# Attention and output projection in one program: the last unit's heads among the products of the first four head groups

## The chip, the cores and the metric

One core of a Trainium2 chip runs the whole program. Its engines work side by side and meet at semaphores: TensorE (PE: matmuls and transposes, results in PSUM banks of 128 x 512 floats), VectorE (DVE), ScalarE (ACT), GpSimd (POOL), and SyncE (SP), which issues the transfers from HBM. The metric is the device time of one execution in microseconds (us), the median of several.

## The reference, cut to what matters

Six residual blocks work on `x`, 8 batches of 32 tokens with 512 values each. The first and the fourth are cross attentions onto a context of 512 tokens per batch; the names of their tiles begin with `c0` and `c1`. One of them computes:

```python
q = (x_norm @ Wq)      # 32 heads of 128
k = (kv @ Wk)          # 8 key/value heads; c0: context and latents, c1: context
v = (kv @ Wv)
q, k = rms_norm(q), rms_norm(k)
probs = softmax(q @ k.T * scale)
out = probs @ v        # 256 tokens x 4096
x = x + out @ Wo       # 4096 x 512
```

The change touches the end of the attention and the last line.

## The kernel before, in words

A full-precision product is three matmuls (`mm3`, lines 51 to 55): each operand is split in a high part (a copy to the rounded type, by ScalarE) and a low part (the difference, by VectorE or GpSimd). So each weight tile and each operand takes a step on ScalarE, then one on a second engine, before TensorE may read it.

`cross_attention` (line 267) runs three programs (blocks), one behind the other, each ended by a barrier of all engines: `queries`, `attend`, `project_out`.

`attend` goes over 16 units: 8 batches with two halves (`hf`) of four key/value heads. A unit has four slots `k`. In a slot TensorE projects the context tile `k` onto keys (bank `kbank[k % 2]`) and values (`vbank`), 12 matmuls each, and between them it works on one head of the unit before: the values of the head before it (`pv`), the scores (`score`), the transposes of the probabilities (`p_transpose`) and of the output (`o_transpose`). The softmax of a head goes over VectorE (maximum), ScalarE (exponential) and back. The output of a head is placed into `qT` by VectorE (`ot_place`, L1028), over the queries that are no longer needed. The order on each engine is written out by hand in its `step`.

The heads of the last unit have no projections left to run among. The function `finish` of each engine takes them in pairs (60 with 61, 62 with 63; `LAST` is 60), with the banks that projections no longer use as second set: `kbanks` for scores, `vbank` for transposed probabilities, `ktbank` for outputs.

The output weights are eight tiles of 128 x 2048 (1 MB), one for each group of four heads, in a ring of four places that the key and value weights leave free (`OutputWeights`, line 325). Tiles 0 and 1 are loaded when the last unit begins, 2 and 3 behind its last value projection. Tiles 0 and 1 are split in `finish`; the low part of tile 0 is made by GpSimd.

`project_out` (line 1104) then takes the groups in order. ScalarE and VectorE split the heads of a group for all 256 tokens (L1135, L1143, 128 x 1024 each) and a tile (L347, L353), and TensorE runs 24 matmuls into two banks, one for each half of the tokens (`t`). At the end VectorE adds both banks to `x` (L1149).

Of the kernel before, what the change touches and what calls it, by code (L numbers as in the profile page):

```python
# [17 lines left out]
ALU = mybir.AluOpType  # L18
# [248 lines left out]
def cross_attention(nc, tag, g, w, eps, latents_as_keys):  # L267

    latents = latents_as_keys
    with ExitStack() as outer:
        so = Space(nc, outer, tag)

        qT = so.sb("qT", [P, B, HEADS, SEQ])
        with ExitStack() as inner:
            si = Space(nc, inner, tag)

            kvw = KeyValueWeights(nc, si, w["wkv"], (0, 1, 2, 3) if latents else (0, 2, 1, 3))
            wkv, wkv_raw = kvw.split, kvw.raw
# [8 lines left out]
            project_out(nc, tag + "o", g, w, qT, wo)  # L291


class Context:
# [30 lines left out]
class OutputWeights:  # L325

    RING = 4
    PLACES = (0, 2, 1, 3)

    def __init__(self, nc, s, src, wkv, wkv_raw):  # L330
        self.nc, self.src, self.wkv, self.wkv_raw = nc, src, wkv, wkv_raw
# [7 lines left out]
    def raw(self, n):  # L339
        return self.wkv_raw[:, self.PLACES[n % self.RING], :]  # L340

    def load(self, sp, n):
        sp.dma_start(self.raw(n), self.src[n]).then_inc(self.loaded[n % self.RING], 16)

    def make_hi(self, act, n):
        act.wait_ge(self.loaded[n % self.RING], 16 * (n // self.RING) + 16)
        self.nc.scalar.activation(self.tile(n)[0], self.raw(n), ACT.Copy).then_inc(self.hi_ready, 1)  # L347

    def make_lo(self, eng, n, subtract):

        eng.wait_ge(self.hi_ready, n + 1)
        hi, lo = self.tile(n)
        subtract(lo, self.raw(n), as_f32(hi), ALU.subtract).then_inc(self.lo_ready, 1)  # L353


def queries(nc, tag, g, w, eps, kvw, qT, klatT, context, vl_stored):
# [262 lines left out]
def attend(nc, tag, g, w, eps, kvw, qT, mask, klatT, vlat, context, wo, vl_stored):  # L619
# [11 lines left out]
    with ExitStack() as ctx:  # L631
# [61 lines left out]
        ot_done = s.sem("ot_done")  # L693
        ot_ready = s.sem("ot_ready")

        scores = [sbank, kbanks]
        ptbanks = [ptbank, vbank]
        obanks = [obank, ktbank]
        LAST = UNIT_H * (UNITS - 1)

        def run(eng, slot_step, finish):

# [15 lines left out]
        with nc.Block() as block:  # L718
            @block.sync
            def _(sp):  # L720
# [24 lines left out]
                def finish():  # L745
                    sp.wait_ge(v_proj, CT * UNITS)
                    for n in range(2, wo.RING):
                        wo.load(sp, n)
                run(sp, step, finish)

            @block.gpsimd
            def _(pool):
# [35 lines left out]
                                            ALU.subtract).then_inc(kl_lo, 1)  # L788

                def finish():  # L790
                    wo.make_lo(pool, 0, nc.gpsimd.tensor_tensor)
                if tail:
                    pool.wait_ge(vl_stored, 32)
                run(pool, step, finish)
# [2 lines left out]
            def _(pe):  # L797
# [98 lines left out]
                            o_transpose(a - 1, (k - 1) % 2, obank)  # L896

                def finish():
                    pe.wait_ge(ot_ready, LAST - 1)
                    pv(LAST - 1, 0, UNIT_H - 1, obank)  # L900
                    wait_unit(UNITS, 1, B)
                    pe.wait_ge(p_ready, LAST)
                    pe.wait_ge(pt_ready, LAST)
                    for k in range(2):
                        score(LAST + k, scores[k], 1, k)
                    o_transpose(LAST - 1, 1, obank)
                    for pair in range(0, UNIT_H, 2):
                        for k in (pair, pair + 1):
                            pe.wait_ge(p_ready, LAST + k + 1)
                            p_transpose(k, ptbanks[k % 2], scores[k % 2])  # L910
                        for k in (pair, pair + 1):

                            pe.wait_ge(ot_ready, LAST + max(0, k - 1))
                            pv(LAST + k, 1, k, obanks[k % 2])
                            if k + 2 < UNIT_H:
                                score(LAST + k + 2, scores[k % 2], 1, k + 2)
                        for k in (pair, pair + 1):
                            o_transpose(LAST + k, k, obanks[k % 2])
                run(pe, step, finish)

            @block.scalar
            def _(act):
# [27 lines left out]
                def step(b, hf):  # L950
                    attends, _, u = parts(b, hf)
                    for k in range(CT):
# [16 lines left out]
                            context.make_hi(act, b + 1, k - 1)  # L969
                        if hf == 0 and k == 0 and not is_at(b, 0):  # L970
                            context.make_hi(act, b, CT - 1)

                def finish():
                    for pair in range(0, UNIT_H, 2):
                        for k in (pair, pair + 1):
                            exponential(LAST + k, k, scores[k % 2])
                        for k in (pair, pair + 1):
                            tail_heads(LAST + k, k, scores[k % 2])
                        wo.make_hi(act, pair // 2)
                run(act, step, finish)  # L980

            @block.vector
            def _(dve):
# [49 lines left out]
                def step(b, hf):  # L1033
                    attends, lags, u = parts(b, hf)
                    for k in range(CT):
# [38 lines left out]
                            context.make_lo(dve, b + 1, k - 1)  # L1074
                        if hf == 0 and k == 0 and not is_at(b, 0):
                            context.make_lo(dve, b, CT - 1)

                def finish():
                    dve.wait_ge(p_ready, LAST)
                    inverse_sum(UNIT_H - 1)  # L1080
                    o_norm(LAST - 1, UNIT_H - 1, obank)
                    for k in range(2):
                        dve.wait_ge(s_done, LAST + k + 1)
                        maximum(LAST + k, k, scores[k])
                    ot_place(LAST - 1, B - 1, 0, UNIT_H - 1, obank)
                    for pair in range(0, UNIT_H, 2):
                        for k in (pair, pair + 1):
                            pt_copy(LAST + k, k, ptbanks[k % 2], scores[k % 2])
                        for k in (pair, pair + 1):
                            dve.wait_ge(p_ready, LAST + k + 1)  # L1090
                            inverse_sum(k)
                            if k + 2 < UNIT_H:
                                dve.wait_ge(s_done, LAST + k + 3)
                                maximum(LAST + k + 2, k + 2, scores[k % 2])
                            o_norm(LAST + k, k, obanks[k % 2])
                        for k in (pair, pair + 1):
                            ot_place(LAST + k, B - 1, 1, k, obanks[k % 2])
                    dve.wait_ge(ot_ready, LAST + UNIT_H)
# [5 lines left out]
def project_out(nc, tag, g, w, oT, wo):  # L1104

    x = g["x"]
    NW = HEADS // GROUP
    HI, LO = 2, 1
    with ExitStack() as ctx:
        s = Space(nc, ctx, tag)  # L1110
        o = s.pair("o", [P, 2, GROUP, TOK])
        ybank = [s.ps(f"ybank{t}") for t in range(TT)]
        o_hi = s.sem("o_hi")
        o_lo = s.sem("o_lo")
        used = s.sem("used")
        added = s.sem("added")

        def heads_of(n):
            return oT[:, :, n * GROUP:(n + 1) * GROUP, :].rearrange("p b h q -> p h b q")

        def split_of(half, n):
            return half[:, n % 2, :, :].rearrange("p h (b q) -> p h b q", b=B)

        with nc.Block() as block:
            @block.sync
            def _(sp):
                for n in range(wo.RING, NW):
                    sp.wait_ge(used, n - wo.RING + 1)
                    wo.load(sp, n)

            @block.scalar
            def _(act):
                for n in range(NW):
                    need(act, used, n - 1)
                    nc.scalar.activation(split_of(o[0], n), heads_of(n), ACT.Copy).then_inc(o_hi, 1)  # L1135
                    if n >= HI:
                        wo.make_hi(act, n)

            @block.vector
            def _(dve):  # L1140
                for n in range(NW):
                    dve.wait_ge(o_hi, n + 1)
                    nc.vector.tensor_tensor(split_of(o[1], n), heads_of(n), as_f32(split_of(o[0], n)),  # L1143
                                            ALU.subtract).then_inc(o_lo, 1)
                    if n >= LO:
                        wo.make_lo(dve, n, nc.vector.tensor_tensor)
                dve.wait_ge(used, NW)
                for t in range(TT):
                    nc.vector.tensor_tensor(x[:, t, :], x[:, t, :], ybank[t][:], ALU.add).then_inc(added, 1)  # L1149
                dve.wait_ge(added, TT)  # L1150

            @block.tensor
            def _(pe):
                for n in range(NW):
                    pe.wait_ge(o_lo, n + 1)
                    pe.wait_ge(wo.lo_ready, n + 1)
                    wt = wo.tile(n)
                    for h in range(GROUP):
                        for t in range(TT):
                            last = mm3(nc, ybank[t][:],  # L1160
                                       tuple(half[:, n % 2, h, t * P:(t + 1) * P] for half in o),
                                       tuple(half[:, h * D:(h + 1) * D] for half in wt),
                                       n == 0 and h == 0, n == NW - 1 and h == GROUP - 1)
                    last.then_inc(used, 1)

# [1243 lines left out]
```

## Time and profile before

| what | us |
|---|---|
| median of 3 runs | 1631.05 |
| the three runs | 1634.22, 1631.05, 1630.61 |
| the profiled execution | 1631.66 |
| its span | 1628.8 |

The profile is of that one execution. Its span runs from the first to the last recorded instruction; the 2.86 us beyond it are start and end. "Idle before" is the time that an engine had nothing under way before an instruction, and what ended it. A matmul's recorded duration is longer than its share of the stream, since matmuls overlap: the step from one start to the next counts. PEld is TensorE's loading of the fixed operand.

### The profile page before, as it was taken

Reading aid. Unit: us, or ns where it says so; the run is one execution under the profiler, and the core shown is the slowest. Engines: PE = TensorE matmul, PEld = TensorE weight load, DVE = VectorE, ACT = ScalarE, POOL = GpSimd, SP = SyncE. Lnnn points to the kernel's source line nnn. Section 1 sums busy time; section 2 is a strip of 40 time slices with the busy share of each in tenths; the row PEclk is TensorE's granted clock in tenths of the full one; section 3 lists DMA queues with packets and bytes.
Section 4 is the critical chain, followed back from the end, with each engine's and each line's share of the span. In section 5 each row is a group of like instructions: output and inputs, shape, how many; then the busy total and the mean of one; then the engine's idle time right before and its main releaser. Section 6 shows DMA issues by size and latency. Waiting matters only on the chain. (4 is left out here: it accounts for less than half of the span.)

```text
span 1628.8 us, 23964 instructions
## 1 busy us (share of the span) xinstructions
PE 1521.6 (93%) x8362; PEld 1293.1 (79%) x8362; DVE 913.2 (56%) x1739; ACT 642.7 (39%) x1184; POOL 335.4 (21%) x494
## 2 busy tenths in 40 slices
PE   7989999999999998897798999999999999875898
PEld 6878888888888886686586888888888887654786
DVE  6835555555555555575584555555555555546665
ACT  5624344343343434363374433333333333421443
POOL 2322222222222221053232211222222121101000
PEclk9999999999999999989899999999999999988899
DMA  8010000000000012273250000000000002210442
GB/s 324 27 62 32 19 18 31 10 31 18 18 31 16 24 58 78 92 262 127 95 189 7 27 14 13 26 6 19 19 6 26 13 13 104 104 72 0 157 157 88
DMA packets 26219, 99.06 MB, mean 61 GB/s; under 512 B 4848, under 2 KB 4976, under 8 KB 20432
## 3 DMA queue, kind: packets, MB, share of 16 engines
q1 hardware_dynamic: 26160, 98.29, 17.0%
q8 instruction: 35, 0.57, 0.1%
q14 instruction: 24, 0.20, 0.0%
HBM read 95.66 MB, written 2.62 MB: 60 GB/s over the span
## 5 line engine op out<-in xcount | busy, mean ns | idle before, releaser
L53 PE MATMUL c0a_kbanks<-c_wkv_lo_r,c_cT_hi 128*128 128x512 f32 x256 | 105.5, 412 | 2.9 <-PEq L408 2.9
L53 PE MATMUL c1a_kbanks<-c_wkv_lo_r,c_cT_hi 128*128 128x512 f32 x256 | 106.4, 416 | 1.2 <-PEq L408 1.2
L1045 DVE TENSOR_REDUCE c1a_ss<-c1a_sq 128x4 f32<-128x512 f32 x64 | 43.9, 686 | 108.2 <-ACT c1a_sq L956 108.2
L55 PE MATMUL c1a_kbanks<-c_wkv_hi,c_cT_lo_r 128*128 128x512 f32 x256 | 101.0, 394 | 0.0
L53 PE MATMUL c0a_vbank<-c_wkv_lo_r,c_cT_hi 128*128 128x512 f32 x256 | 100.6, 393 | 0.0
L55 PE MATMUL c0a_kbanks<-c_wkv_hi,c_cT_lo_r 128*128 128x512 f32 x256 | 100.5, 393 | 0.0
L54 PE MATMUL c1a_kbanks<-c_wkv_hi,c_cT_hi 128*128 128x512 f32 x256 | 100.5, 392 | 0.0
L54 PE MATMUL c0a_vbank<-c_wkv_hi,c_cT_hi 128*128 128x512 f32 x256 | 100.4, 392 | 0.0
L1045 DVE TENSOR_REDUCE c0a_ss<-c0a_sq 128x4 f32<-128x512 f32 x64 | 43.9, 685 | 100.3 <-ACT c0a_sq L956 93.6
L54 PE MATMUL c0a_kbanks<-c_wkv_hi,c_cT_hi 128*128 128x512 f32 x256 | 100.0, 391 | 0.0
L55 PE MATMUL c1a_vbank<-c_wkv_hi,c_cT_lo_r 128*128 128x512 f32 x256 | 100.0, 391 | 0.0
L53 PE MATMUL c1a_vbank<-c_wkv_lo_r,c_cT_hi 128*128 128x512 f32 x256 | 99.9, 390 | 0.0
L55 PE MATMUL c0a_vbank<-c_wkv_hi,c_cT_lo_r 128*128 128x512 f32 x256 | 99.8, 390 | 0.0
L54 PE MATMUL c1a_vbank<-c_wkv_hi,c_cT_hi 128*128 128x512 f32 x256 | 99.6, 389 | 0.0
L1016 DVE COPY c0a_pT<-c0a_ptbank 128x512 f32<-128x512 f32 x62 | 42.9, 692 | 98.2 <-PE c0a_sbank L824 98.2
L938 ACT ACTIVATE c1a_p<-c1a_sm,c1a_nmax 128x512 f32<-128x512 f32 x64 | 46.4, 724 | 128.4 <-DVE c1a_nmax L1003 128.4
L770 POOL TENSOR_TENSOR c1a_ms<-c1a_ss,c1a_const 128x4 f32<-128x4 f32 x64 | 12.7, 199 | 397.7 <-DVE c1a_ss L1045 397.7
L938 ACT ACTIVATE c0a_p<-c0a_sbank,c0a_nmax 128x544 f32<-128x544 f32 x62 | 44.3, 715 | 125.9 <-DVE c0a_nmax L996 125.9
L770 POOL TENSOR_TENSOR c0a_ms<-c0a_ss,c0a_const 128x4 f32<-128x4 f32 x64 | 12.8, 200 | 393.3 <-DVE c0a_ss L1045 393.3
L956 ACT ACTIVATE c1a_sq<-c1a_kbanks 128x512 f32<-128x512 f32 x64 | 38.2, 597 | 125.5 <-PE c1a_kbanks L55 125.5
L1016 DVE COPY c1a_pT<-c1a_ptbank 128x512 f32<-128x512 f32 x62 | 42.9, 691 | 75.1 <-PE c1a_ptbank L821 75.0
L956 ACT ACTIVATE c0a_sq<-c0a_kbanks 128x512 f32<-128x512 f32 x64 | 38.2, 597 | 118.3 <-PE c0a_kbanks L55 118.3
(469 smaller groups left out, 4388.0 us busy)
## 6 DMA issues: line engine op xcount, KB each, us to landing
g_stage<-in_l_wq SPq DMA_DIRECT2D x16, 1024.0 KB, 5.4
c_cT_lo<-in_ctx SPq DMA_DIRECT2D x64, 256.0 KB, 2.5
c_wkv_lo<-in_l_wo SPq DMA_DIRECT2D x16, 1024.0 KB, 4.7
e_stage<-in_e_w SPq DMA_DIRECT2D x20, 768.0 KB, 4.2
c_wkv_lo<-in_l_wkv SPq DMA_DIRECT2D x8, 1024.0 KB, 7.8
m_stage<-in_mix_ffn SPq DMA_DIRECT2D x10, 768.0 KB, 5.3
c_vlat<-vlat_dram SPq DMA_DIRECT2D x32, 64.0 KB, 1.9
m_traw<-in_mix_out SPq DMA_DIRECT2D x1, 1792.0 KB, 12.0
```

The source lines that it names most:

```text
L53: nc.tensor.matmul(out, a[0], b[1], start=start, stop=False)
L54: nc.tensor.matmul(out, a[0], b[0], start=False, stop=False)
L55: return nc.tensor.matmul(out, a[1], b[0], start=False, stop=stop)
L770: nc.gpsimd.tensor_tensor(ms[:, k % 2, :], ss[:, k % 2, :], const[:, 1, :], ALU.add).then_inc(k_mean, 1)
L938: nc.scalar.activation(dst, src, ACT.Exp, bias=nmax[:, k:k + 1], accum_out=rsum[:, k:k + 1]).then_inc(p_ready, 1)
L956: nc.scalar.activation(sq[:], kbank[k % 2], ACT.Square, scale=HD ** -0.5).then_inc(k_squared, 1)
L1016: last = nc.vector.tensor_copy(pT[:, k % 2, :, :], bank[:, :].rearrange("p (t n) -> p t n", t=CT))
L1045: nc.vector.tensor_reduce(ss[:, k % 2, :], sq[:, :].rearrange("p (h d) -> p h d", h=UNIT_H), AX.X, ALU.add).then_inc(k_summed, 1)
```

## The change

`project_out` is gone, with its block and its barrier. Its work is the new class `OutputProjection`, run within `attend`. The work of a group is cut in two by tokens, which gives 16 products of 12 matmuls, in the order `PARTS`: for groups 0 to 3 both token halves in turn, then groups 4 to 7 for the first half of the tokens, then for the second. The bank of the first half is `kbank[0]`, of the second `kbank[1]`. The split heads lie in the four places of the context tiles (`c_cT_hi`, `c_cT_lo`), 128 x 512 each.

In the last unit's slots ScalarE and VectorE also split three halves of weight tiles and two token splits (`last_unit`, `WO_LAST_UNIT`). In `finish` the heads no longer go in pairs: each runs alone, with product 2j ahead of its scores and 2j+1 behind them, and behind each head stand as many halves of weight tiles as `WO_FINISH` says (half i belongs to tile i // 2). GpSimd has nothing left there. A product waits for its split heads and for both halves of its tile.

```diff
+    PARTS = [(n, t) for n in range(4) for t in range(TT)] + [(n, t) for t in range(TT) for n in range(4, 8)]
+    RING = 4
...
+    def make_hi(self, act, q):
+        n, t = self.PARTS[q]
+        last = (t + 1) * BT - 1
+        if q < self.RING:
+            act.wait_ge(self.v_proj, CT * (UNITS - 1) + q + 1)
+        else:
+            act.wait_ge(self.used, q - self.RING + 1)
+        act.wait_ge(self.ot_ready, UNIT_H * (2 * last + n // UNIT_H) + n % UNIT_H + 1)
+        self.nc.scalar.activation(self.place(self.split[0], q), self.heads(q), ACT.Copy).then_inc(self.o_hi, 1)
...
+    def product(self, pe, q):
+        n, t = self.PARTS[q]
+        pe.wait_ge(self.o_lo, q + 1)
+        self.wo.wait_tile(pe, n)
+        wt = self.wo.tile(n)
+        for h in range(GROUP):
+            last = mm3(self.nc, self.ybank[t], tuple(half[:, q % self.RING, h * P:(h + 1) * P] for half in self.split),
+                       tuple(half[:, h * D:(h + 1) * D] for half in wt),
+                       n == 0 and h == 0, n == self.wo.NW - 1 and h == GROUP - 1)
+        last.then_inc(self.used, 1)
...
+        WO_LAST_UNIT = ((), (0,), (1,), (2,))
+        WO_FINISH = ((3,), (4, 5, 6), (7, 8, 9), (10, 11))
...
+                    for n in range(wo.RING, wo.NW):
+                        sp.wait_ge(out.used, TT * (n - wo.RING + 1))
                         wo.load(sp, n)
...
                 def finish():
-                    pe.wait_ge(ot_ready, LAST - 1)
-                    pv(LAST - 1, 0, UNIT_H - 1, obank)
...
+                    for j in range(UNIT_H):
+                        a = LAST + j
+                        _, lhf, lk = unit_before(j)
+                        pe.wait_ge(k_normed, CT * UNITS - 1)
+                        out.product(pe, 2 * j)
+                        pe.wait_ge(ot_ready, a - 1)
+                        pv(a - 1, lhf, lk, obank)
...
+                        score(a, sbank, 1, j)
+                        pe.wait_ge(k_normed, CT * UNITS)
+                        out.product(pe, 2 * j + 1)
+                        pe.wait_ge(p_ready, a + 1)
+                        p_transpose(j, ptbank, sbank)
+                        o_transpose(a - 1, lk % 2, obank)
+                    out.product(pe, 2 * UNIT_H)
...
                 def finish():
...
+                    for j in range(UNIT_H):
+                        exponential(LAST + j, j, sbank)
+                        for q in (2 * j + 2, 2 * j + 3):
+                            out.make_hi(act, q)
+                        tail_heads(LAST + j, j, sbank)
+                        for i in WO_FINISH[j]:
+                            wo.make_hi(act, i)
...
                 def finish():
...
+                        maximum(a, j, sbank)
+                        o_norm(a - 1, lk, obank)
+                        for q in (2 * j + 2, 2 * j + 3):
+                            out.make_lo(dve, q)
+                        pt_copy(a, j, ptbank, sbank)
+                        ot_place(a - 1, lb, lhf, lk, obank)
+                        for i in WO_FINISH[j]:
+                            wo.make_lo(dve, i)
```

How the order moves, in c0. VectorE, in the finish, before: from the scores of the first pair of heads to the probabilities of the second of them. `c0a_nmax` is the maximum, `c0a_pT` the copied probabilities, `c_qT` the placed output.

```order
L996 TENSOR_REDUCE c0a_nmax<-c0a_sbank 128x1
L996 TENSOR_REDUCE c0a_nmax<-c0a_kbanks 128x1
L1028 COPY c_qT<-c0a_obank 128x128
L1016 COPY c0a_pT<-c0a_ptbank 128x512
L1020 TENSOR_TENSOR c0a_pT_stack<-c0a_sbank,c0a_pT_stack 32x128
L1016 COPY c0a_pT<-c0a_vbank 128x512
L1020 TENSOR_TENSOR c0a_pT_stack<-c0a_kbanks,c0a_pT_stack 32x128
```

VectorE at the same place after the change: head 61. `c_cT_lo_r` is now the low part of the split heads (line 398), `c_wkv_lo_r` that of the output weights (line 358).

```order
L1081 RECIPROCAL c0a_rinv<-c0a_rsum 128x1
L1085 TENSOR_REDUCE c0a_nmax<-c0a_sbank 128x1
L1099 TENSOR_SCALAR c0a_on<-c0a_obank,c0a_rinv 128x128
L398 TENSOR_TENSOR c_cT_lo_r<-c_qT,c_cT_hi 128x512 x2
L1105 COPY c0a_pT<-c0a_ptbank 128x512
L1109 TENSOR_TENSOR c0a_pT_stack<-c0a_sbank,c0a_pT_stack 32x128
L1117 COPY c_qT<-c0a_obank 128x128
L358 TENSOR_TENSOR c_wkv_lo_r<-c_wkv_lo,c_wkv_hi 128x1024 x3
```

The second head's work is gone from the piece; two token splits and three weight halves have come in, the halves behind the placing of the output. Before, the weight parts of VectorE all stood in the next block.

TensorE at the turn from one head of the finish to the next, after the change: the end of product 2j+1, the transposes, the beginning of product 2j+2 (each product is 12 rows, these three in turn four times).

```order
L55 MATMUL c0a_kbanks<-c_wkv_hi,c_cT_lo_r 128x512
L894 MATMUL c0a_ptbank<-g_ident,c0a_p 128x128 x4
L897 MATMUL c0a_sbank<-g_ident,c0a_p 32x128
L915 MATMUL c0a_obank<-g_ident,c0a_on 128x128
L53 MATMUL c0a_kbanks<-c_wkv_lo_r,c_cT_hi 128x512
```

TensorE before, where the finish ended and the products began:

```order
L842 MATMUL c0a_obank<-g_ident,c0a_on 128x128
L842 MATMUL c0a_ktbank<-g_ident,c0a_on 128x128
L718 UNCONDITIONAL_BRANCH
L1152 UNCONDITIONAL_BRANCH
L53 MATMUL c0o_ybank<-c_wkv_lo_r,c0o_o_hi 128x512
```

The first eight products have moved in among the heads, so that `L915`, the output's transpose, now stands directly ahead of a product four times over.

## Rows read from the trace of the kernel before

**Rows 1.** The page: busy time of each engine, share of the span.

```profile
PE 1521.6 (93%) x8362; PEld 1293.1 (79%) x8362; DVE 913.2 (56%) x1739; ACT 642.7 (39%) x1184; POOL 335.4 (21%) x494
```

**Rows 2.** Busy time by stretch: last projections, finish, products; c0, then c1.

```profile
core 0: us, PE busy (x) PEld busy (x) DVE busy (x) ACT busy (x) POOL busy (x), PEclk, DMA share, GB/s
604.00:617.20 13.20, 13.20 (x80) 11.53 (x79) 6.66 (x14) 4.48 (x10) 2.42 (x4) 1.00 0.00 1
617.20:638.80 21.60, 13.61 (x106) 11.70 (x104) 13.23 (x33) 12.80 (x24) 4.54 (x1) 0.96 0.26 99
638.80:685.60 46.80, 46.80 (x192) 37.33 (x192) 24.38 (x14) 17.20 (x12) 0.00 (x0) 0.95 0.25 90
...
1375.70:1395.80 20.10, 12.21 (x83) 9.73 (x81) 12.01 (x36) 10.05 (x14) 4.57 (x1) 0.98 0.27 105
1395.80:1442.60 46.80, 46.77 (x191) 37.48 (x192) 24.42 (x14) 17.20 (x12) 0.00 (x0) 0.94 0.26 90
```

**Rows 3.** Waits of PE, us 616 to 710: total, times, longest.

```profile
PE c0o_ybank L53 <- DVE c0o_o_lo L1143: 3.2, 1, 3.2
PE c0a_obank L832 <- DVE c_qT L1028: 1.6, 1, 1.6
PE c0a_ktbank L842 <- DVE c0a_on L1010: 1.3, 2, 1.0
```

**Rows 4.** Timeline of c0: start us, us, engine, instruction [idle before, releaser].

```profile
625.01 0.27 PE L824 MATMUL c0a_kbanks<-g_ident,c0a_p 128*32 128x128 f32 x1
...
625.32 0.56 ACT L947 ACTIVATE c0a_pT_stack<-c0a_kbanks 32x128 fp32r<-32x128 f32 x2 [0.19 <-PE c0a_kbanks L824]
...
625.90 1.92 ACT L347 ACTIVATE c_wkv_hi<-c_wkv_lo 128x2048 fp32r<-128x2048 f32 x1
...
638.79 0.80 PE L53 MATMUL c0o_ybank<-c_wkv_lo_r,c0o_o_hi 128*128 128x512 f32 x1 [3.22 <-DVE c0o_o_lo L1143]
...
644.00 0.39 PE L53 MATMUL c0o_ybank<-c_wkv_lo_r,c0o_o_hi 128*128 128x512 f32 x1
...
646.75 0.39 PE L53 MATMUL c0o_ybank<-c_wkv_lo_r,c0o_o_hi 128*128 128x512 f32 x1
```

**Rows 5.** Stretches around three pauses, columns as in rows 2 (PEclk: granted clock).

```profile
888.00:898.00 10.00, 7.10 (x35) 5.69 (x35) 5.12 (x6) 4.60 (x7) 1.77 (x3) 1.00 0.00 0
635.60:638.80 3.20, 0.01 (x1) 0.01 (x1) 1.58 (x3) 2.00 (x2) 0.00 (x0) 0.73 0.03 8
638.80:644.00 5.20, 5.20 (x13) 4.10 (x13) 3.27 (x2) 0.00 (x0) 0.00 (x0) 0.51 0.00 0
1395.80:1401.80 6.00, 5.97 (x14) 4.70 (x15) 3.31 (x2) 0.00 (x0) 0.00 (x0) 0.51 0.01 3
```

**Rows 6.** Groups of DVE by form, us 617 to 705: busy, mean ns.

```profile
L996 DVE TENSOR_REDUCE c0a_nmax<-c0a_sbank 128x1 f32<-128x544 f32 x2 | 1.4, 724 | 1.4 <-PE c0a_sbank L811 1.4
L137 DVE TENSOR_TENSOR m_xT_lo<-m_tbank,m_xT_hi 128x512 fp32r<-128x512 f32 x2 | 1.3, 686 | 2.3 <-ACT m_xT_hi L163 2.3
L1149 DVE TENSOR_TENSOR g_x<-g_x,c0o_ybank 128x512 f32<-128x512 f32 x2 | 1.3, 684 | 5.9 <-PE c0o_ybank L55 5.9
L1282 DVE TENSOR_TENSOR m_pw_lo<-m_praw,m_pw_hi 128x1024 fp32r<-128x1024 f32 x1 | 1.2, 1215 | 0.0
L1028 DVE COPY c_qT<-c0a_obank 128x128 f32<-128x128 f32 x4 | 1.1, 280 | 0.0
```

**Rows 7.** Groups of ACT by form, the same stretch.

```profile
L938 ACT ACTIVATE c0a_p<-c0a_sbank,c0a_nmax 128x544 f32<-128x544 f32 x2 | 1.4, 714 | 4.5 <-DVE c0a_nmax L996 4.5
L1280 ACT ACTIVATE m_pw_hi<-m_praw 128x1024 fp32r<-128x1024 f32 x1 | 1.1, 1058 | 15.3 <-DMA m_disc<-in_mix_disc 15.3
L961 ACT ACTIVATE c0a_v<-c0a_vbank 128x512 f32<-128x512 f32 x1 | 0.6, 597 | 1.1 <-PE c0a_vbank L55 1.1
```

**Rows 8.** Timeline of PE: a pause after which the clock held.

```profile
894.12 0.66 PE L848 MATMUL c1a_ktbank<-g_ident,c1a_kn 128*128 128x128 f32 x4 [2.90 <-DVE c1a_kn L1061]
```

**Rows 9.** DMA issues of the whole run: KB each, median us to landing.

```profile
c_wkv_lo<-in_l_wo SPq DMA_DIRECT2D x16, 1024.0 KB, 4.7
```

More of the change, by code:

```diff
@@ L349, in make_lo @@
[L349 to L353, printed above, removed]
+        self.nc.scalar.activation(self.half(self.tile(n)[0], i), self.half(self.raw(n), i),
+                                  ACT.Copy).then_inc(self.hi_ready, 1)
+    def make_lo(self, dve, i):
+        hi, lo = self.tile(i // 2)
+        dve.wait_ge(self.hi_ready, i + 1)
+        self.nc.vector.tensor_tensor(self.half(lo, i), self.half(self.raw(i // 2), i), as_f32(self.half(hi, i)),
+                                     ALU.subtract).then_inc(self.lo_ready, 1)
@@ L694, in attend, with last_unit, unit_before @@
         ot_ready = s.sem("ot_ready")
-        scores = [sbank, kbanks]
-        ptbanks = [ptbank, vbank]
-        obanks = [obank, ktbank]
         LAST = UNIT_H * (UNITS - 1)
+        out = OutputProjection(nc, s, g["x"], qT, wo, context, kbank, ot_ready, v_proj)
+        PARTS = len(out.PARTS)
+        WO_LAST_UNIT = ((), (0,), (1,), (2,))
+        WO_FINISH = ((3,), (4, 5, 6), (7, 8, 9), (10, 11))
+        def last_unit(b, hf):
+            return is_at(b, B - 1) and hf == 1
+        def unit_before(j):
+            return (B - 1, 1, j - 1) if j else (B - 1, 0, UNIT_H - 1)
         def run(eng, slot_step, finish):
@@ L898, in finish @@
                 def finish():
-                    pe.wait_ge(ot_ready, LAST - 1)
-                    pv(LAST - 1, 0, UNIT_H - 1, obank)
[L901 to L918, printed above, removed]
+                    for j in range(UNIT_H):
[5 more added lines that the diff above has]
+                        pv(a - 1, lhf, lk, obank)
+                        if j == 0:
+                            wait_unit(UNITS, 1, B)
+                        pe.wait_ge(p_ready, a)
+                        pe.wait_ge(pt_ready, a)
+                        score(a, sbank, 1, j)
[4 more added lines that the diff above has]
+                        o_transpose(a - 1, lk % 2, obank)
@@ L919, in _ @@
+                    out.product(pe, 2 * UNIT_H)
+                    pe.wait_ge(ot_ready, LAST + UNIT_H - 1)
+                    pv(LAST + UNIT_H - 1, 1, UNIT_H - 1, obank)
+                    out.product(pe, 2 * UNIT_H + 1)
+                    o_transpose(LAST + UNIT_H - 1, (UNIT_H - 1) % 2, obank)
+                    for q in range(2 * UNIT_H + 2, PARTS):
+                        out.product(pe, q)
                 run(pe, step, finish)
@@ L971, in step @@
                             context.make_hi(act, b, CT - 1)
-                def finish():
[L974 to L979, printed above, removed]
+                        if last_unit(b, hf):
+                            for i in WO_LAST_UNIT[k]:
+                                wo.make_hi(act, i)
+                            if k >= 2:
+                                out.make_hi(act, k - 2)
+                def finish():
+                    for j in range(UNIT_H):
[4 more added lines that the diff above has]
+                        for i in WO_FINISH[j]:
+                            wo.make_hi(act, i)
+                    for n in (6, 7):
+                        for i in (2 * n, 2 * n + 1):
+                            wo.make_hi(act, i)
+                        out.make_hi(act, n + 4)
+                    for q in range(12, PARTS):
+                        out.make_hi(act, q)
                 run(act, step, finish)
@@ L1101, in _ @@
                 run(dve, step, finish)
[L1104 to L1164, printed above, removed]
```

78 lines of the change are left out of this document (55 added, 23 removed).

## The prediction

> **What bounds the kernel now.** I read the page first: TensorE is busy for 93% of the span, VectorE for 56%, ScalarE for 39% [rows 1]. A change therefore pays only where TensorE stands still or runs at its lower clock. The chain that ended last is no help, since it covers only the last stage. So I cut the trace into stretches around the place that the change rewrites, once in each cross attention (c0 and c1) [rows 2]. The last unit's projections keep TensorE busy without a break (13.20 of 13.20 us). Then comes the finish, 21.6 us in c0 and 20.1 us in c1, in which it is busy for 13.61 and 12.21 us: 8.0 and 7.9 us idle. Then come 46.8 us of output projection, busy all the time, with a mean clock of 0.95 and 0.94. The two idle stretches and the lost clock are all that the change can win.
>
> The list of waits splits the idle time of c0 [rows 3]: 3.2 us before the first product, for the split of the heads behind the block boundary, and 1.6 us, 1.3 us and shorter ones within the heads. The timeline shows the clock's part [rows 4]. The first product's matmuls start 0.43 us apart at the lower level (1.2 GHz), later ones 0.229 us at the upper one (2.4 GHz). The first twelve, 638.79 to 644.00, take 5.21 us, the next twelve, to 646.75, take 2.75: **a fall of the clock costs 2.5 us**. In c1 fourteen take 6.0 us [rows 5] instead of 14 x 0.229 = 3.2: 2.8 us. The clock was at 0.73 in the 3.2 us before, so 2 x 0.27 x 3.2 = 1.7 us of the fall lay in the pause, and at 0.51 for the 5.2 us after: some 6.8 us in all [rows 5].
>
> **What moves, TensorE.** The 192 matmuls of each projection and those of the last unit's heads stay as many and as large; only their order changes. A product of 12 matmuls is 2.75 us. For each head j TensorE now runs product 2j, the heads' values of j-1, the scores of j, product 2j+1, the transposes of j and that of the output of j-1. The softmax of head j (maximum 0.72, exponential 0.71 [rows 6, 7]) lies under product 2j+1: with 0.3 us for hand-overs and the reading of the sum 1.7 us against 2.75. These waits go.
>
> **The wait that comes in.** Product 2j+2 needs the next tile of output weights in both halves. The order on VectorE shows where the low halves stand: behind the copy of the probabilities and the placing of the output, and the placing waits for the transpose that is TensorE's last instruction before that product. So the halves can't be made under TensorE's work; it stands until they are done. For c0 the chain behind the transposes of head 0, from the rows: ScalarE copies the tail (starts 0.04 us after them, at 625.32 in the row, and takes 0.58 to the next instruction [rows 4]), splits one half of the tile (128x1024, 1.06 [rows 7]), VectorE subtracts it (1.22 [rows 6]), and 0.1 us for the two hand-overs: 3.0 us, less the 0.1 us by which the output's transpose ends later. A pause of **2.9 us**. Behind head 1 stand three halves, of which product 4 wants two: one more step of VectorE (1.22 less the overlap of 0.09): **4.0 us**. Behind head 2 product 6 wants one half: 2.9 us again. Behind head 3 the halves are there in time; before product 9 0.3 us are left, and product 10 waits for the placing of the last output and one token split behind it (0.28 + 0.69 + hand-over): 1.0 us. In c1 there is no tail. There VectorE is bound: it comes from the two token splits 0.5 us after the transposes, then copy 0.6, placing 0.2, half 1.22: 2.55 us, 3.7 us, 2.55 us, then 1.0 us. A token split of 512 columns is in no row: it lies between 0.28 us (128 columns) and 1.22 us (1024); I take 0.69 us for VectorE and 0.60 us for ScalarE, the rows of other work with 512 columns [rows 6, 7]. With the lower end the pauses of c1 shorten by some 0.4 us a split, with the upper one those of both layers grow by as much; the three of c0 never fall below ScalarE's chain.
>
> **The sum at the upper clock.** c0: pauses 11.1 us (2.9 + 4.0 + 2.9 + 0.3 + 1.0) in place of 8.0: +3.1. The fall of now is taken off to be counted anew: -2.5. Each restart also costs 0.2 us in which TensorE's records still count as busy, and there are three fewer: -0.6. Together 0.0. c1: 9.8 in place of 7.9, +1.9, -2.8, -0.6: -1.5. The first addition to x (two of 0.68 us [rows 6]) now runs under the products of the second half of the tokens: -0.6 in each. All: **-2.7 us**.
>
> **The clock again.** Each layer now has three pauses of 2.55 to 4.0 us instead of one of 3.2. The rows say of pauses: after 3.2 us of waiting the first product ran at the lower level, in both layers; after a pause of 2.90 us in c1 the matmuls ran on at full speed, and the clock was 1.00 throughout [rows 5, 8]. So I count the long pause of each layer as a fall, and each of the four shorter, which have transposes at low load in front of them, as one in four or less: 1.5 falls in c0 and, with its pauses 0.35 us shorter, 1.25 in c1. At 2.65 us, the mean of the two measured, that is 7.3 us. The bounds of one fall are 0 (it lies wholly within a pause) and 3.2 us (all 6.8 us lie on products: 6.8 / 0.43 = 16 matmuls, 0.2 us each).
>
> **What costs nothing.** In the last unit's slots VectorE gets three weight halves and two token splits (3 x 1.22 + 2 x 0.69 = 5.0 us over four slots of 8.3 us) and ScalarE 3 x 1.06 + 2 x 0.60 = 4.4 us; both are busy for about half of such a slot [rows 2], which hides them. If that cover were gone, each would push a projection by its own length. SP issues the same eight tiles, each earlier. Tiles 2 and 3 are issued at 617.4 as now, land 4.7 us later [rows 9] and are first read after 636 us; tile 7 goes out behind product 7 and is wanted some 5 us later. GpSimd loses its one subtraction (4.54 us), on which nobody waited.
>
> **Result.** The profiled execution took 1631.66 us (span 1628.8). -2.7 + 7.3 = +4.6 gives 1636.3 us; it lies 0.6 above the median of the three runs, so on the median's scale **1635.7 us**. A measurement of this kernel can tell about 0.2%, 3.3 us, from no change.
>
> **Rivals.**
> 1. *Only the long pause of each layer falls.* -2.7 + 2 x 2.65 = +2.6: 1633.7 us, within 0.2%. For it: the shorter pauses are no longer than the 2.9 us that kept the clock. Against it: transposes stand ahead of them. The Trainium skill (TensorE: Matmul & The Clock Gate, Why this matters for your kernels) asks for no idle gaps of over about 3 us between bursts of matmuls; by that rule this rival is the case, at 1633.7 us.
> 2. *The clock holds.* This is the other side: -2.7 us, 1628.3 us, not slower. It decides at one point: whether pauses of 3.7 and 4.0 us keep the clock. The fall after 3.2 us, twice, speaks against it. For it speaks that TensorE works densely between the new pauses (7 us) where now the whole finish is thin.
> 3. *Every pause falls.* Six falls instead of 2.75: -2.7 + 15.9 = +13.2, 1644 us.
> 4. *The products cover the chains, as the code means to.* Then the idle 8.0 and 7.9 us, both falls, the restarts and additions go, some 11.5 us a layer: 1608 us. It needs the weight halves ahead of the placing on VectorE; the order there says otherwise.
>
> **How the numbers follow.** The forecast (two to four falls) has 0.45, rival 1 0.20, rival 2 0.12, rival 3 0.13, rival 4 0.05, and 0.05 are for a pause or split that I mis-sized. Slower by over 0.2% are most of the forecast (0.42), rival 3 and a little of the rest: 0.57. Within 0.2%: rivals 1 and 2 and the low end of the forecast, 0.35. Faster by over 0.2%: rival 4 and an undersized gain, 0.08. The range reaches from rival 2 to just short of rival 3: 1628.5 to 1643 us.
>
> **What would show it.** In the new trace TensorE waits before product 2, 4 and 6 of each layer for a low half of the weights (VectorE, the line of that subtraction), for about 2.9, 4.0 and 2.9 us in c0 and 0.3 us less in c1, and not for exponentials. Behind the 4 us wait matmuls start 0.43 us apart. The first addition to x ends before the last products. Finish and products together take 21.6 + 46.8 = 68.4 us in c0 now, and I expect 72.4; in c1 66.9 and 68.7. I am wrong if those waits are under 2 us, if the clock reads 1.00 over the finish, or if another engine or a DMA ends them.

## The result: slower by 0.36%

The changed kernel takes **1638.9 us** in the median (1630.3 to 1642.1, 20 runs), the kernel before 1631.95 us (1629.6 to 1635.7, 20 runs beside them). The ratio is 1.0036, with a 95% interval of 1.0025 to 1.0047: 5.9 us slower (4.1 to 7.7). The spread is part of the result. It is 6 us before and 12 us after, and it goes with the clock granted over the whole run: the quickest run of after (1630.32 us) had a mean of 0.974, the slowest (1642.14 us) of 0.966. 0.008 of some 1635 us is 13 us more of lost clock, against 11.8 us more time.

The profiled execution took 1633.11 us (span 1631.2, clock 0.972), 5.8 us under the median and only 1.45 us above the profiled one of before. It shows where TensorE stands still. Of the clock's falls it shows one sample, and a mild one: its mean clock was 0.972, that of the median run 0.968.

The page of after has the row that answers to the one of before [rows 1]:

```profile
PE 1520.4 (93%) x8362; PEld 1294.4 (79%) x8362; DVE 917.8 (56%) x1773; ACT 645.0 (40%) x1216; POOL 326.3 (20%) x492
```

The list of waits of TensorE in after, core 0: first from 616 to 689 us (the finish and products of c0), then from 1370 to 1446 us (c1). The columns are total us, times, longest:

```profile
PE c0a_kbanks L53 <- DVE c_wkv_lo_r L358: 10.5, 4, 4.1
PE c0a_kbanks L53 <- DVE c_cT_lo_r L398: 1.0, 1, 1.0
...
PE c1a_kbanks L53 <- DVE c_wkv_lo_r L358: 8.6, 3, 3.6
PE c1a_kbanks L53 <- DVE c_cT_lo_r L398: 1.0, 1, 1.0
```

No wait for an exponential or for the normed output is left. Those of before [rows 3] are gone, and in their place TensorE waits for the low half of the output weights (L358), and once in each layer for a token split (L398). The timeline around the first turn, from TensorE's last transpose of head 0 to product 2:

```profile
625.87 0.27 PE L915 MATMUL c0a_obank<-g_ident,c0a_on 128*128 128x128 f32 x1
626.07 0.56 ACT L1024 ACTIVATE c0a_pT_stack<-c0a_sbank 32x128 fp32r<-32x128 f32 x2 [0.61 <-PE c0a_sbank L897]
...
626.65 1.06 ACT L352 ACTIVATE c_wkv_hi<-c_wkv_lo 128x1024 fp32r<-128x1024 f32 x1
...
627.19 0.29 DVE L1117 COPY c_qT<-c0a_obank 128x128 f32<-128x128 f32 x1
627.74 1.22 DVE L358 TENSOR_TENSOR c_wkv_lo_r<-c_wkv_lo,c_wkv_hi 128x1024 fp32r<-128x1024 f32 x1 [0.26 <-ACT c_wkv_hi L352]
...
629.12 0.47 PE L53 MATMUL c0a_kbanks<-c_wkv_lo_r,c_cT_hi 128*128 128x512 f32 x1 [2.97 <-DVE c_wkv_lo_r L358]
```

That is the chain of the prediction link by link: ScalarE's copy of the tail, its split of the half, VectorE's subtraction, and 2.97 us on TensorE. VectorE itself waits 0.26 us for ScalarE. The last unit's slots hide their new work: TensorE is still busy for 13.20 of the 13.20 us from 604.00 to 617.20.

The busy time by stretch, after (columns: stretch, its length, then PE, PEld, DVE, ACT and POOL busy, the granted clock, the DMA share and GB/s):

```profile
617.20:688.80 71.60, 60.08 (x296) 49.55 (x294) 37.90 (x62) 28.73 (x49) 0.00 (x0) 0.95 0.24 89
629.10:636.20 7.10, 7.08 (x31) 6.00 (x32) 0.71 (x3) 0.00 (x0) 0.00 (x0) 0.76 0.06 25
655.60:662.00 6.40, 6.36 (x35) 5.60 (x36) 3.21 (x5) 1.30 (x4) 0.00 (x0) 1.00 0.09 38
1378.70:1445.80 67.10, 57.41 (x275) 46.79 (x273) 36.51 (x65) 25.86 (x39) 0.00 (x0) 0.97 0.26 94
1389.80:1396.00 6.20, 6.11 (x24) 5.06 (x25) 0.00 (x0) 0.00 (x0) 0.00 (x0) 0.72 0.19 79
1402.90:1410.10 7.20, 7.16 (x36) 6.02 (x37) 2.43 (x7) 1.55 (x4) 0.00 (x0) 1.00 0.02 5
```

Finish and products of c0 together take 71.6 us (68.4 before, from the sum of two stretches [rows 2]), those of c1 67.1 (66.9). The work right behind a pause ran at a clock of 0.76 behind the first of c0 (3.0 us), and at 0.72 behind the first of c1, which lasted only 2.5 us. It ran at 1.00 behind the third of c0 (3.0 us) and behind the longest of c1 (3.6 us). The length of a pause does not tell whether the clock falls. Behind the 4.1 us it fell, as the timeline of TensorE shows by the distance of the starts:

```profile
642.95 0.47 PE L53 MATMUL c0a_kbanks<-c_wkv_lo_r,c_cT_hi 128*128 128x512 f32 x1 [4.10 <-DVE c_wkv_lo_r L358]
643.48 0.60 PE L55 MATMUL c0a_kbanks<-c_wkv_hi,c_cT_lo_r 128*128 128x512 f32 x1
...
646.87 0.42 PE L54 MATMUL c0a_kbanks<-c_wkv_hi,c_cT_hi 128*128 128x512 f32 x1
```

The first two matmuls run at the upper level. Then the eight steps from the start at 643.48 to that at 646.87 take 3.39 us, 0.42 each, the lower level (1.2 GHz). At 0.229 they would take 1.83: this fall cost 1.6 us, not the 2.5 and 2.8 of the two in before.

### The profile page after: what moved, and what is told of

It reads as the page before. It is cut to its first block and busy times, and to the rows that moved or that the text cites. A ratio compares the mean times of both kernels' runs of the same rounds, so it can differ in the third digit from the quotient of the medians.

```text
span 1631.2 us, 24066 instructions
## 1 busy us (share of the span) xinstructions
PE 1520.4 (93%) x8362; PEld 1294.4 (79%) x8362; DVE 917.8 (56%) x1773; ACT 645.0 (40%) x1216; POOL 326.3 (20%) x492
## 5 line engine op out<-in xcount | busy, mean ns | idle before, releaser
L53 PE MATMUL c0a_kbanks<-c_wkv_lo_r,c_cT_hi 128*128 128x512 f32 x320 | 132.6, 415 | 14.4 <-DVE c_wkv_lo_r L358 10.5
L53 PE MATMUL c1a_kbanks<-c_wkv_lo_r,c_cT_hi 128*128 128x512 f32 x320 | 132.7, 415 | 10.7 <-DVE c_wkv_lo_r L358 8.6
L55 PE MATMUL c1a_kbanks<-c_wkv_hi,c_cT_lo_r 128*128 128x512 f32 x320 | 126.7, 396 | 0.0
L55 PE MATMUL c0a_kbanks<-c_wkv_hi,c_cT_lo_r 128*128 128x512 f32 x320 | 126.7, 396 | 0.0
L54 PE MATMUL c0a_kbanks<-c_wkv_hi,c_cT_hi 128*128 128x512 f32 x320 | 126.2, 394 | 0.0
L54 PE MATMUL c1a_kbanks<-c_wkv_hi,c_cT_hi 128*128 128x512 f32 x320 | 126.0, 394 | 0.0
```

What stands on the lines that cost most here:

```text
L53: nc.tensor.matmul(out, a[0], b[1], start=start, stop=False)
L54: nc.tensor.matmul(out, a[0], b[0], start=False, stop=False)
L55: return nc.tensor.matmul(out, a[1], b[0], start=False, stop=stop)
```

## The experiments

All are compared with the kernel before, run beside them on the same chip (median 1632.5 us in both batches, 21 and 22 runs). Where two changed kernels are compared, it is by the difference of their ratios; the two intervals together leave such a difference open by 2.3 to 3.5 us either way. The theory: the halves of the weight tiles stand too late and make the pauses, and the pauses cost a second time through the clock. The rivals: it is the amount of work and not its place; the clock has no part; only the long pauses bring it down.

**The halves one head ahead**

```diff
-        WO_LAST_UNIT = ((), (0,), (1,), (2,))
-        WO_FINISH = ((3,), (4, 5, 6), (7, 8, 9), (10, 11))
+        WO_LAST_UNIT = ((), (0, 1), (2,), (3,))
+        WO_FINISH = ((4, 5), (6, 7), (8, 9), (10, 11))
```

> The changed kernel with the low and high halves of the output weights made one head earlier: halves 0 and 1 in slot 1 of the last unit, 2 in slot 2, 3 in slot 3, then (4, 5), (6, 7), (8, 9), (10, 11) behind the four heads. Same instructions, other order. Theory (the pauses before products 2, 4 and 6 are VectorE's low halves behind the placing, and the clock falls in them): the three pauses of 2.4 to 4.0 us go in both layers, 9.9 and 8.2 us, and with them all falls in the finish; the pauses of 1.0 us before product 10 stay. About 1611 us, 21 below the kernel before. Rival 1 (ScalarE and VectorE lack the room, so the halves made earlier delay maximum, copy or the next head instead): pauses of about the same sum move to the values or transposes, 1630 us or more. Rival 2 (the loss lies outside the pauses, in products cut by tokens or in the last unit's fuller slots): at most 3 us below the changed kernel.

Measured: 1609.9 us (1609.0 to 1616.7, 5 runs), ratio 0.9876 (0.9857 to 0.9894). The waits of TensorE in the finish and products, c0 (616 to 674.9 us) and c1 (1370 to 1421.3 us), where these are all that the lists hold:

```profile
PE c0a_kbanks L53 <- DVE c_cT_lo_r L398: 1.0, 1, 1.0
PE c0a_kbanks L53 <- DVE c_wkv_lo_r L358: 0.4, 1, 0.4
...
PE c1a_kbanks L53 <- DVE c_cT_lo_r L398: 1.0, 1, 1.0
```

The same turn in its timeline: product 2 starts 0.03 us after the transpose does. VectorE's subtraction starts at 627.71, as it did in after (627.74), but it now makes the half of a later product.

```profile
625.83 0.27 PE L915 MATMUL c0a_obank<-g_ident,c0a_on 128*128 128x128 f32 x1
625.86 0.47 PE L53 MATMUL c0a_kbanks<-c_wkv_lo_r,c_cT_hi 128*128 128x512 f32 x1
...
627.71 1.23 DVE L358 TENSOR_TENSOR c_wkv_lo_r<-c_wkv_lo,c_wkv_hi 128x1024 fp32r<-128x1024 f32 x1 [0.27 <-ACT c_wkv_hi L352]
```

The stretch of the finish and products of c0 (in c1 the clock is 1.00 as well, over 1366.00 to 1421.40 us):

```profile
617.20:674.90 57.70, 56.20 (x295) 47.16 (x293) 36.78 (x61) 27.76 (x48) 0.00 (x0) 1.00 0.31 110
```

c0 takes 57.7 us in place of 71.6, with the same matmuls and a clock of 1.00. The same halves and splits are made by the same engines; one more of them in the last unit's slots costs nothing that can be seen. So neither the amount of work nor the form of the change is at fault, but the place of the halves: 3, 4, 5 and 7 of the finish stand one place earlier, and so do 1 and 2 within the last unit. Against after it is 0.0160 of 1632 us, 26.1 us. The waits account for 18.7 of them: 10.5 + 1.0 + 8.6 + 1.0 = 21.1 in after, 1.0 + 0.4 + 1.0 = 2.4 here. Some 7 us are left for the clock.

**The pauses filled with unused matmuls**

```diff
                         o_transpose(a - 1, lk % 2, obank)
+                        for _ in range((10, 14, 10, 0)[j]):
+                            nc.tensor.matmul(vbank[:, 0:CTX], kT[0][:, 1, j, 0:P], kT[0][:, 1, j, 0:CTX],
+                                             start=True, stop=True)
```

> The changed kernel with 10, 14 and 10 matmuls of 512 columns onto a bank that nobody reads, put on TensorE behind the output's transpose of heads 60, 61 and 62, where it waits anyway (2.3, 3.2 and 2.3 us of work in pauses of 2.9, 4.0, 2.9 us in c0 and 2.4, 3.5, 2.4 us in c1). They compute nothing that is used. Theory (part of the loss is the clock): granted clock 1.00 over the whole finish and all products, median about 1629 us, 9 or 10 below the changed kernel and 3 below the kernel before, and runs that lie closer together. Rival (the pauses alone cost the time, falls are short or come anyway): within 2 us of the changed kernel, 1637 to 1641 us.

Measured: 1629.75 us (1626.8 to 1634.6, 11 runs), ratio 0.9985 (0.9973 to 0.9996). Against after's 1.0036 that is 0.0051, **8.3 us** (5.7 to 10.9) for the clock alone, since the products start no sooner: from the output's transpose of head 0 to product 2 it is 3.25 us in both (625.63 to 628.88 here, 625.87 to 629.12 in after). The stretches of c0 at the same places of the work, and the finish and products of c1, now with the pause full and a clock of 1.00 everywhere:

```profile
616.90:685.50 68.60, 64.83 (x330) 53.40 (x328) 37.94 (x62) 28.90 (x49) 0.00 (x0) 1.00 0.26 92
626.10:629.10 3.00, 2.32 (x11) 1.63 (x10) 2.32 (x4) 1.33 (x2) 0.00 (x0) 1.00 0.97 317
629.10:636.20 7.10, 7.10 (x39) 6.07 (x39) 1.43 (x4) 1.74 (x4) 0.00 (x0) 1.00 0.05 17
1375.00:1443.00 68.00, 65.95 (x319) 53.61 (x317) 38.31 (x70) 26.70 (x41) 0.91 (x1) 1.00 0.26 93
```

This kernel is also the measurement of the sum at the upper clock: 0.0015 of 1632.5, 2.4 us faster than before (0.7 to 4.4). One part of the expectation did not come true: the runs do not lie closer together, they spread over 7.8 us.

**The wait of the kernel before, filled**

```diff
             def _(pe):
+                pe.wait_ge(wo.hi_ready, 1)
+                for _ in range(10):
+                    nc.tensor.matmul(ybank[0][:], wo.tile(0)[0][:, 0:P], wo.tile(0)[0][:, 0:D],
+                                     start=True, stop=True)
                 for n in range(NW):
                     pe.wait_ge(o_lo, n + 1)
```

> The kernel before with 10 matmuls of 512 columns onto the first product's bank at the head of the projection block, where TensorE waits 3.2 us; they compute nothing that is used. Theory (one fall of the clock of 2.5 and 2.8 us in each layer): clock 1.00 over the first products, 4 to 5.5 us below the kernel before, about 1627 us. Rival (the clock falls because the whole finish is thin, not because of this pause): it falls all the same, within 1 us of the kernel before.

Measured: 1630.6 us (1627.8 to 1632.5, 11 runs), ratio 0.9988 (0.9979 to 0.9997): 2.0 us faster (0.5 to 3.4), half or less of the 4 to 5.5 expected. The place itself did what it should. The clock is 1.00 over the wait and the first products, where before had 0.73 and 0.51 [rows 5]:

```profile
635.60:642.80 7.20, 6.49 (x28) 5.26 (x29) 4.74 (x4) 2.01 (x2) 0.00 (x0) 1.00 0.02 3
1393.40:1401.80 8.40, 7.57 (x33) 6.13 (x34) 4.85 (x4) 2.01 (x2) 0.00 (x0) 1.00 0.01 3
893.00:896.40 3.40, 2.90 (x9) 2.52 (x10) 1.31 (x3) 1.55 (x2) 0.29 (x1) 0.50 0.02 5
```

The last row is elsewhere in the program, in code that is not touched. There the kernel before ran at the upper level:

```profile
893.00:896.40 3.40, 2.27 (x12) 1.97 (x13) 1.39 (x3) 1.54 (x2) 0.91 (x2) 1.00 0.00 0
```

The stretch at 893 is the pause of 2.90 us in c1 that had kept the clock in before [rows 5, 8]. Here the clock fell at it, and once more from 766.8 to 773.5 us (0.50, where before has 1.00; the work there stands 2.4 us later in before). Over the whole execution the mean clock was 0.972 against 0.971: most of what was saved at the two filled places was lost at others. That the filling moved the falls is not shown by this. The same pause in c1, 2.88 to 2.90 us in all nine profiled executions, is followed by a fall in four of them, and one is that of the next experiment, where nothing is filled (0.83 over 10 us):

```profile
902.00:912.00 10.00, 7.12 (x29) 5.63 (x28) 5.00 (x6) 3.81 (x6) 1.77 (x3) 0.83 0.01 2
```

So the clock in untouched code differs from one execution to the next. The mean clock of the median run fits the small gain: 0.972 here, 0.971 before, which is 1.6 us of full clock against 2.0 us of time. Why it is not 4 to 5.5 stays open.

**Two halves behind each head: the pauses made longer**

```diff
-        WO_LAST_UNIT = ((), (0,), (1,), (2,))
-        WO_FINISH = ((3,), (4, 5, 6), (7, 8, 9), (10, 11))
+        WO_LAST_UNIT = ((), (0,), (1,), ())
+        WO_FINISH = ((2, 3), (4, 5), (6, 7), (8, 9, 10, 11))
```

> The changed kernel with one more half left behind each placing: (2, 3), (4, 5), (6, 7), (8, 9, 10, 11) in the finish, halves 0 and 1 alone in the last unit. Theory: products 2, 4, 6 and 8 each wait 4.0 us in c0 and 3.5 us in c1, 16 and 14 us a layer instead of 9.9 and 8.2 us, so 6 us more a layer, and the clock falls in nearly every one, 2 to 3 us more a layer: about 1655 us. Rival (the pauses are set by something else, the scores or a transfer): less than 5 us above the changed kernel.

Measured: 1654.95 us (1653.1 to 1658.1, 4 runs), ratio 1.014 (1.012 to 1.016). Four waits for L358 in each layer, the only others being those of 1.0 us for L398; c0 from 616 us, c1 from 1385 us:

```profile
PE c0a_kbanks L53 <- DVE c_wkv_lo_r L358: 16.4, 4, 4.1
...
PE c1a_kbanks L53 <- DVE c_wkv_lo_r L358: 14.4, 4, 3.6
```

The waits are 11.7 us longer than in after (30.8 against 19.1), the time 17 us (1.0140 - 1.0036 = 0.0104 of 1632), so some 5 us more went to the clock. The stretches behind the first of the four pauses of 4.1 us in c0, and behind the first, third and fourth of those of 3.6 us in c1:

```profile
631.40:638.00 6.60, 6.50 (x29) 5.56 (x30) 0.12 (x2) 0.00 (x0) 0.00 (x0) 0.74 0.00 1
...
1401.10:1408.00 6.90, 6.77 (x22) 5.60 (x23) 0.00 (x0) 0.00 (x0) 0.00 (x0) 0.56 0.02 7
...
1429.30:1436.00 6.70, 6.54 (x33) 5.58 (x34) 1.23 (x6) 0.94 (x3) 0.00 (x0) 1.00 0.02 7
1440.80:1447.00 6.20, 6.06 (x24) 5.00 (x25) 2.89 (x5) 5.37 (x7) 0.00 (x0) 0.72 0.01 3
```

Each pause of 4.1 us brought a fall (0.74 to 0.75 over such a stretch for all four). Behind the four of 3.6 us, equal to 0.02 us, there were in turn a long fall (0.56), a long one (0.58), none, and a shorter one (0.72).

**The halves ahead of the copy and the placing**

```diff
-                        tail_heads(LAST + j, j, sbank)
                         for i in WO_FINISH[j]:
                             wo.make_hi(act, i)
+                        tail_heads(LAST + j, j, sbank)
...
-                        pt_copy(a, j, ptbank, sbank)
-                        ot_place(a - 1, lb, lhf, lk, obank)
                         for i in WO_FINISH[j]:
                             wo.make_lo(dve, i)
+                        pt_copy(a, j, ptbank, sbank)
+                        ot_place(a - 1, lb, lhf, lk, obank)
```

> The changed kernel with the weight halves of the finish ahead of the copy of the probabilities and the placing on VectorE, and ahead of the tail's copy on ScalarE; as many halves, behind the same heads. Theory (the place behind the placing makes the pauses): the halves no longer wait for TensorE's last transpose. From the end of the scores ScalarE needs exponential 0.71 behind a maximum of 0.72, two token splits of 0.6 and a half of 1.06 (3.7 us), VectorE 1.22 more (5.0 us with hand-over), TensorE's product and transposes 3.25 us: pauses of about 1.75, 2.95 and 1.75 us in place of 2.86, 4.00 and 2.86, some 3 us less in each layer, and with shorter pauses fewer falls of the clock: about 1630 us. Rival (the amount of work on VectorE between two heads makes the pauses, wherever it stands): the pauses stay at 3 to 4 us, now for the copy of the probabilities, and the time stays at 1639 us.

Measured: 1631.2 us (1627.4 to 1632.6, 12 runs), ratio 0.9992 (0.9982 to 1.0001). Against after it is 0.0044, 7.2 us. The waits, c0 to 686.9 us and c1 to 1440.9 us:

```profile
PE c0a_kbanks L53 <- DVE c_wkv_lo_r L358: 6.1, 3, 2.8
PE c0a_obank L905 <- DVE c_qT L1117: 1.6, 2, 1.2
...
PE c1a_kbanks L53 <- DVE c_wkv_lo_r L358: 7.0, 3, 3.1
...
PE c1a_obank L905 <- DVE c_qT L1117: 0.9, 1, 0.9
```

In c0 the three waits come to 6.1 us, the longest 2.8, where 1.75 + 2.95 + 1.75 = 6.45 were expected. Against after that is 4.4 us less, more than the 3 expected; in c1 (7.0 us, the longest 3.1) it is only 1.6 less. And 2.5 us of these 6.0 come back as waits for the placing (L1117), which is now behind the halves. 7.2 - 3.5 = 3.7 us are then left for the clock, which reads 1.00 over the finish and products of both layers in this profile. So the order within a head is worth 7 us and makes the change as quick as the kernel before; the order between heads is worth 26.

**The token split of product 10 ahead of the last placing**, in the version with the halves one head ahead

```diff
-                        if n == 6:
-                            ot_place(LAST + UNIT_H - 1, B - 1, 1, UNIT_H - 1, obank)
                         out.make_lo(dve, n + 4)
+                        if n == 6:
+                            ot_place(LAST + UNIT_H - 1, B - 1, 1, UNIT_H - 1, obank)
```

> The version with the halves one head ahead (one_head_ahead, 1609.9 us), and in it the token split of product 10 on VectorE ahead of the placing of the last output, on which that product does not depend. Theory: the last wait of 1.0 us before product 10 goes, in both layers, and nothing takes its place: 2 us less, about 1608 us. Rival (product 10 waits for its weight halves just as long): 1.0 us stays before it, now for the subtraction of the weights, and the time stays at 1609.9 us.

Measured: 1610.4 us (1608.3 to 1610.7, 4 runs), ratio 0.987 (0.985 to 0.988), which can't be told from the 1609.9 us without it. The waits shrink as foreseen, from 1.0 to 0.2 us in c0 and to 0.4 us in c1:

```profile
PE c0a_kbanks L53 <- DVE c_cT_lo_r L398: 0.2, 1, 0.2
...
PE c1a_kbanks L53 <- DVE c_cT_lo_r L398: 0.4, 1, 0.4
```

That is 1.4 us of waiting, under what four or five runs can show. Inconclusive in time.

**Only the longest pause filled**

```diff
-                        for _ in range((10, 14, 10, 0)[j]):
+                        for _ in range((0, 14, 0, 0)[j]):
```

(the first line is that of the kernel with all pauses filled)

> The changed kernel with 14 more matmuls of 512 columns (their results are not used) in the pause before product 4 alone, of 4.0 us in c0 and 3.5 us in c1; the shorter pauses (2.9 and 2.4 us) stay empty. Theory (any of the pauses can bring the clock down, the short ones too): falls are still seen behind pauses of 2.4 to 2.9 us, and about two thirds of the 9 us that filling all of them gave back are still lost: 1633 to 1637 us. Rival (only pauses of over 3 us bring a fall, as the rule of about 3 us in the Trainium skill, TensorE: Matmul & The Clock Gate, has it): no fall in the finish or the products, and 1629.8 us, as with all pauses filled.

Measured: 1637.5 us (1635.0 to 1638.1, 11 runs), ratio 1.0030 (1.0021 to 1.0039), 0.5 us over the upper end of what was expected. Filling the longest pause of each layer gave back 0.0006, 1 us, which is within the intervals (at most 3.3); filling the two shorter ones as well gives back the other 7.3 (1.0030 - 0.9985 = 0.0045). The stretches behind the two pauses left in c0, and behind the two in c1; of the second pause of c0 the row of the pause itself too:

```profile
632.60:639.00 6.40, 6.40 (x35) 5.58 (x36) 1.04 (x3) 0.83 (x3) 0.00 (x0) 1.00 0.10 38
653.00:656.00 3.00, 0.03 (x2) 0.06 (x1) 2.70 (x6) 2.95 (x5) 0.00 (x0) 0.86 0.82 276
656.00:662.20 6.20, 6.20 (x18) 5.09 (x19) 2.10 (x2) 0.46 (x1) 0.00 (x0) 0.52 0.09 36
...
1394.80:1400.00 5.20, 5.20 (x21) 4.29 (x21) 0.00 (x0) 0.00 (x0) 0.00 (x0) 0.67 0.21 90
...
1418.10:1424.00 5.90, 5.82 (x30) 4.98 (x31) 3.36 (x7) 0.24 (x2) 0.00 (x0) 1.00 0.20 85
```

One of the two pauses of 3.0 us and one of the two of 2.5 us brought the clock down, the former with nearly its whole fall on the product behind it: (1 - 0.52) x 6.2 = 3.0 us lost. The rival, by which only pauses of over 3 us count, is refuted.

## Why the prediction was right

The forecast was 1635.7 us, 4.6 us slower; measured are 5.9 by the ratio (7.0 by the medians). The pauses were right in cause and size. The clock's term was right in its sum, but not in how it was made up, so that part of the agreement is luck. Point by point:

- **The pauses.** Right in place, cause and size. Forecast 2.9 + 4.0 + 2.9 + 0.3 us in c0, 10.1, measured 10.5 in four waits, the longest 4.1. Forecast 2.55 + 3.7 + 2.55 in c1, 8.8, measured 8.6, the longest 3.6. Forecast 1.0 before product 10, measured 1.0. That they come from the place of the halves is shown from three sides: one head ahead and they are gone, ahead of the placing and they are 6.0 us shorter, two behind each head and all four are of 4.1 us (3.6 in c1).
- **The sum at the upper clock.** Forecast -2.7 us. The kernel with its pauses filled, which has no fall in this place, is at -2.4 (-4.4 to -0.7).
- **The clock.** Forecast 2.75 falls at 2.65 us, +7.3. Between the kernel with empty and with full pauses lie 8.3 us (5.7 to 10.9): the size fits, its make-up does not. Two of the 2.75 falls, 5.3 us, were put on the long pause of each layer; filling those two gave back 1 us, at most 3.3 (unless falls came at the other pauses instead, which one profile can't tell). The cost of a fall is no constant either: 1.6 us in the eight steps above, 3.0 behind the second pause of c0 in the last experiment. So 8.3 us can be three falls or five, and where they lie in the median run no profile shows; the profiled one had two in c0 and one in c1 and was 5.8 us under the median. The prediction took the pause of 2.90 us that kept the clock [rows 5, 8] as a sign of what such pauses do. It was one draw: the same pause is followed by a fall in four of nine executions.
- **The stretches.** Forecast 72.4 us for finish and products of c0 and 68.7 for c1, measured 71.6 and 67.1. The pauses in them fit; what is short of the forecast is the clock, 0.8 and 1.6 us, in this mild execution.
- **What costs nothing.** As foreseen, one addition of c0 runs under the products (at 679.16 us) and one behind them (688.76 us):

```profile
679.16 0.68 DVE L414 TENSOR_TENSOR g_x<-g_x,c0a_kbanks 128x512 f32<-128x512 f32 x1
688.76 0.69 DVE L414 TENSOR_TENSOR g_x<-g_x,c0a_kbanks 128x512 f32<-128x512 f32 x1 [8.93 <-PE c0a_kbanks L55]
```

  The token split, for which I had only bounds, takes 0.68 to 0.69 us on VectorE (675.90 and 678.55 us in the same timeline), against 0.69 assumed.
- **The rivals.** Rival 1 (only the long pause falls, 1633.7 us) is refuted by the last experiment. The rule of the Trainium skill (TensorE: Matmul & The Clock Gate, Why this matters for your kernels), no idle gaps of over about 3 us, does not hold here as a sharp bound: pauses of 2.5 us behind transposes brought falls, one in after and one in the last experiment. Whether the transposes ahead of a pause (six in c0, five in c1, some 0.8 us) count towards it was not tested. Rival 2 (the clock holds, 1628.3 us) describes the filled kernel, not this one; the quickest of the 20 runs, 1630.3 us, comes near it. Rival 3 (every pause falls) is contradicted by the pauses above that kept the clock. Rival 4 (the products cover the chains, 1608 us) did not come true for this order. Its price was right, the version one head ahead is at 1609.9 us, but its condition was not: with the halves ahead of the placing, as it asked, the kernel is at 1631.2 us and still waits 6.1 and 7.0 us for them. It took a lead of a whole head.

## What to carry to other kernels

When work is moved between products to fill TensorE, the operands of the next product should be made one turn ahead, behind nothing that waits for TensorE's last instruction before it: here the same instructions gave +5.9 us in one order and -20 us in the other. Read a software pipeline from the consumer back: what stands directly ahead of the producer in its engine's queue, and what does that wait for? And count a new pause of TensorE of 2.5 us or more as possibly more than its length: 19 us of waiting, nearly all in six pauses, cost another 8 us of clock here, and unused matmuls in the pause are a cheap test that splits the two.

## What was not expected of the hardware

- **Equal pauses, different clock.** Tallied over the profiled executions of after and of the experiments with open pauses in the finish: behind pauses of 4.1 us the clock fell in 5 of 5, behind 3.6 us in 3 of 5, behind 3.0 us in 2 of 4, behind 2.5 us in 2 of 4. In the version with the halves ahead of the placing it held behind the longest of each layer (2.8 and 3.1 us); the stretch behind the latter:

```profile
1397.10:1404.00 6.90, 6.83 (x34) 5.84 (x35) 3.09 (x8) 1.23 (x3) 0.00 (x0) 1.00 0.09 37
```

  Nor is it a matter of the edits. The nine programs do the same work up to the last unit of c0, and in all of them TensorE has a pause of 2.94 to 2.98 us that ends at about 92 us. In six the clock held there; in three it fell (0.78, 0.80 and 0.86 over 86 to 96 us). The stretch in after, and in the version with the halves ahead of the placing:

```profile
86.00:96.00 10.00, 7.06 (x33) 5.51 (x32) 2.08 (x3) 2.67 (x5) 0.14 (x2) 1.00 0.47 187
86.00:96.00 10.00, 7.05 (x26) 5.41 (x25) 2.08 (x3) 2.20 (x4) 0.14 (x2) 0.78 0.41 162
```

  So from such rows a forecast can give a chance per pause, and one execution that kept the clock proves little.
- **Falls come in two sizes.** The work behind a pause ran at 0.51 to 0.58 over 5 to 7 us in some cases and at 0.67 to 0.76 over such stretches in others. The larger size cost 2.5 to 3.0 us, the smaller 1.6 in the one that was counted out.
- **More spread.** The changed kernel spread over 12 us from run to run, twice that of before, and the time of a run could be read off its mean clock. That open pauses make the spread is not shown: with four of the six open, 11 runs spread over 3.0 us, and with all filled, 11 runs over 7.8.
